# Cross attention on one core: two groups of Q ahead of a tile of V, the mask turned one tile later, and the last products by row blocks

## What is computed

```
qh = split_heads(q @ wq.T + bq)
kh = split_heads(k @ wk.T + bk)
vh = split_heads(v @ wv.T + bv)
scores = einsum('ntd,nsd->nts', qh, kh) / sqrt(depth) + mask * PAD
ctx = einsum('nts,nsd->ntd', softmax(scores), vh)
out = merge_heads(ctx) + q
out = (out - mean(out)) / sqrt(var(out) + 1e-5) * gamma + beta
```

## Time and profile before

| | |
|---|---|
| median of 3 runs | 1091.9 us (1089.82 to 1092.0) |
| the profiled execution | 1091.3 us |
| its span | 1089.2 us |
| TensorE products busy | 1064.5 us, 98% |
| VectorE busy | 939.8 us, 86% |
| GpSimd busy | 773.8 us, 71% |
| ScalarE busy | 725.4 us, 67% |

### The profile page before, as it was taken

How to read it: one execution, slowest core, us unless ns; L and a number is a source line. 1 busy time by engine, 2 the same in 40 slices (tenths; PEclk the granted TensorE clock), 3 DMA queues, 4 the chain that set the end, 5 groups by cost and what they waited for, 6 DMA issues and landing times.

```text
span 1089.2 us, 27000 instructions
## 1 busy us (share of the span) xinstructions
PE 1064.5 (98%) x7541; PEld 978.4 (90%) x7541; DVE 939.8 (86%) x1778; ACT 725.4 (67%) x1149; POOL 773.8 (71%) x685
## 2 busy tenths in 40 slices
PE   7999899999999999999999999999999999999995
PEld 7888789999999999999999999999999999999994
DVE  5989878888888898888888888888888888888897
ACT  3331566777777777777777777777777777777674
POOL 3999723776777777777777777777777777777687
PEclk9999999999999999999999999999999999999998
DMA  7664645465565565555566566566555556556444
...
DMA packets 176905, 171.32 MB, mean 157 GB/s; under 512 B 110004, under 2 KB 111556, under 8 KB 176868
## 3 DMA queue, kind: packets, MB, share of 16 engines
...
...
## 4 chain that ended last, share of the span: by engine, by line
PE 85%; POOL 7%; DVE 4%; issue 1%; DMA 1%; ACT 1%; SPq 1%; DVEq 0%; ACTq 0%; POOLq 0%
PE q_ps L950 33%; PE o_ps L1035 24%; PE t_ps L998 13%; PE s_ps L982 11%; PE s_ps L985 4%; POOL k_part L323 2%; POOL k_shift L319 2%; POOL v_out L335 1%; PE o_ps L965 1%; DMA keep_h<-in_mask 1%; POOL x_lo L354 0%; DVE stats L1107 0%; POOL wq_lo L350 0%; DVE row_max L1173 0%; DVE attn L1099 0%
## 5 line engine op out<-in xcount | busy, mean ns | idle before, releaser
L1035 PE MATMUL o_ps<-v_tiles,pt 128*128 128x66 f32 x2500 | 307.3, 270 | 0.5 <-DVE attn L1099 0.5
L1035 PEld LDWEIGHTS o_ps<-v_tiles,pt 128*128 128x128 f32 x2500 | 298.7, 192 | 0.9 <-issue 0.9
L1426 ACT COPY pt<-t_ps 128x512 f32<-128x512 f32 x315 | 184.0, 584 | 153.2 <-PE t_ps L998 150.2
L1173 DVE TENSOR_REDUCE row_max<-s_ps 128x8 f32<-128x616 f32 x256 | 204.6, 799 | 91.2 <-PE s_ps L985 80.3
L1302 POOL TENSOR_TENSOR x_lo<-xT_raw,x_hi 128x512 fp32r<-128x512 f32 x120 | 153.3, 1278 | 178.7 <-ACT x_hi L1399 178.0
L1389 ACT ACTIVATE probs<-probs 128x616 f32<-128x616 f32 x256 | 184.2, 720 | 82.5 <-DVE probs L1182 76.8
L950 PE MATMUL q_ps<-x_lo,wq_hi 128*128 128x512 f32 x496 | 221.2, 446 | 0.0
L1260 POOL TENSOR_TENSOR attn<-attn,v_late 128x512 f32<-128x512 f32 x124 | 159.5, 1287 | 74.4 <-DVE attn L1099 74.2
L1182 DVE TENSOR_TENSOR probs<-s_ps,row_max 128x616 f32<-128x616 f32 x256 | 204.6, 799 | 5.8
L950 PE MATMUL q_ps<-x_hi,wq_hi 128*128 128x512 f32 x496 | 195.7, 395 | 0.0
L950 PE MATMUL q_ps<-x_hi,wq_lo 128*128 128x512 f32 x496 | 195.5, 394 | 0.0
...
## 6 DMA issues: line engine op xcount, KB each, us to landing
xT_raw<-in_xT SPq DMA_DIRECT2D x128, 256.0 KB, 3.5
...
k_scratch<-k_out SPq DMA_DIRECT2D x8, 1232.0 KB, 5.5
...
```

Source lines behind the costliest of these rows:

```text
L1035: mm = pe.matmul(bank_of(b, t)[:, col:col + tile_cols[i]], pt_of(b, h)[0:w, i, P * t:P * t + P], v_tiles[v_buffer(b, h)][0:w, i, 0:tile_co ...
L1173: dve.tensor_reduce(row_max[:, u, :].rearrange("p (j h) -> p j h", j=2), score_heads(t), AX.X, ALU.max).then_inc(max_ready, 1)
L1426: act.copy(pt[h][0:w, i, :], t_ps[0:w, :]).then_inc(pt_ready, 1)
```

## The change

Three things are moved, and one is joined.

1. `turn_keep` comes behind value tile 1 of chunk 0 instead of tile 0.
2. On TensorE the first two groups of Q of batch 0 come ahead of the last chunk's value tile, and take the banks of groups 48 and 49 instead of 52 and 53. ScalarE reads them out ahead of the casts of key tiles 28 and 29, issues the moves there, and makes x's high parts between the last casts. VectorE makes Q's first low parts behind the low part of tile 28.
3. In the tail the two halves of a row block follow each other (`in_turn`), half 0 in one bank and half 1 in the other (`bank_of`).
4. The row factors of batch 30 are computed once for its four row blocks. ScalarE copies x into PSUM ahead of the normalizations.

```diff
+def first_group(g):
+    return CHUNKS * GROUPS + g - (VT - LATE if g < 2 else 0)
-    return bank(CHUNKS * GROUPS + g)
+    return bank(first_group(g))
...
             n = (2 * c + half) * NG + m
-            if n == 2 * NG * CHUNKS - 1:
+            behind_end = 2 * NG * CHUNKS - n
+            if behind_end == 4:
                 first_high(0)
+            if behind_end == 3:
                 first_high(1)
                 move_first_half()
+            if behind_end == 2:
+                second_x(0)
+                second_x(1)
+            if behind_end == 1:
+                second_x(2)
+                second_x(3)
             act.wait_ge(k_ready, n + 1)
...
+    def second_x(k):
+        if k == 0:
+            act.wait_ge(k_done, 2 * NG * CHUNKS)
+        act.wait_ge(xT_loaded[k], 2 * DMA)
+        act.copy(x_hi1[:, k, :], xT_raw[:, k, :]).then_inc(x_hi_ready, 1)
...
-    act.wait_ge(k_done, 2 * NG * CHUNKS)
-    for k in range(KC):
-        act.wait_ge(xT_loaded[k], 2 * DMA)
-        act.copy(x_hi1[:, k, :], xT_raw[:, k, :]).then_inc(x_hi_ready, 1)
     first_high(2)
...
-        for j in range(VT if c < CHUNKS - 1 else LATE):
+        if c == CHUNKS - 1:
+            last_values(c)
+            return
+        for j in range(VT):
             bias_values(c, j)
             if j < NG:
                 low_keys_out(2 * c * NG + NG + j)
-        if c < CHUNKS - 1:
-            return
-        for j in range(LATE, NG):
-            if j == NG - 1:
-                for g in range(2):
-                    first_low(g)
-            low_keys_out(2 * c * NG + NG + j)
+    def last_values(c):
+        first = 2 * c * NG + NG
+        bias_values(c, 0)
+        low_keys_out(first)
+        first_low(0)
+        first_low(1)
+        low_keys_out(first + 1)
+        low_keys_out(first + 2)
         for k in range(2):
             dve.wait_ge(x_hi_ready, KC + k + 1)
             dve.tensor_tensor(x_lo1[:, k, :], xT_raw[:, k, :], x_hi1[:, k, :], ALU.subtract
                               ).then_inc(x_lo_ready, 1)
+        low_keys_out(first + 3)
...
-        wait_for_bank(pe, CHUNKS * GROUPS + g)
+        wait_for_bank(pe, first_group(g))
...
         ctx_part = (ctx_hi[c % 2], ctx_lo[c % 2])
+        if c == CHUNKS - 1:
+            for g in range(2):
+                first_queries(g)
...
-            if (c, j) == (0, 0):
+            if (c, j) == (0, 1):
                 turn_keep()
-    for g in range(NG):
+    for g in range(2, NG):
         first_queries(g)
...
-def bank_of(b, t):
-    return t_ps if is_last(b) and t % 2 == 0 else o_ps
+def bank_of(b, h):
+    return t_ps if is_last(b) and h == 0 else o_ps
+def in_turn(b, h, t):
+    return 2 * t + h if is_last(b) else 4 * h + t
...
         if is_last(b):
-            u = 4 * h + t
+            u = in_turn(b, h, t)
             if u > 0:
                 pe.wait_ge(attn_ready, b * 8 + (u - 1))
...
     tail_turn(0)
     product(LAST, 0, 0)
     tail_turn(1)
-    product(LAST, 0, 1)
-    product(LAST, 0, 2)
-    product(LAST, 0, 3)
-    tail_turn(2)
-    product(LAST, 1, 0)
-    tail_turn(3)
-    for t in range(1, TT):
+    for t in range(TT):
         product(LAST, 1, t)
+        if t + 1 < TT:
+            product(LAST, 0, t + 1)
+        if t + 2 < TT:
+            tail_turn(t + 2)
...
     read_out(LAST - 1, 1, 3, 1 - LAST_PAR)
     read_out(LAST, 0, 0, LAST_PAR)
-    read_out(LAST, 0, 1, LAST_PAR)
-    tail_stats(LAST - 1, 2, 1 - LAST_PAR)
-    read_out(LAST, 0, 2, LAST_PAR)
-    tail_stats(LAST - 1, 3, 1 - LAST_PAR)
-    read_out(LAST, 0, 3, LAST_PAR)
+    for t in range(2, TT):
+        tail_stats(LAST - 1, t, 1 - LAST_PAR)
     for t in range(TT):
         read_out(LAST, 1, t, LAST_PAR)
         add_last_row(t)
+        if t + 1 < TT:
+            read_out(LAST, 0, t + 1, LAST_PAR)
         tail_stats(LAST, t, LAST_PAR)
...
     add_rows(LAST - 1, 3, 1 - LAST_PAR)
-    tail_factors(LAST - 1, 0, 2, 3)
-    scale_rows(LAST - 1, 0, 1 - LAST_PAR)
-    tail_factors(LAST - 1, 2, 4, 4)
-    scale_rows(LAST - 1, 1, 1 - LAST_PAR)
-    scale_rows(LAST - 1, 2, 1 - LAST_PAR)
+    tail_factors(LAST - 1, 0, TT, 3)
+    for t in range(TT - 1):
+        scale_rows(LAST - 1, t, 1 - LAST_PAR)
...
     copy_tail(0)
     exponent(LAST, 1, 3)
     copy_tail(1)
-    norm(LAST - 1, 0, 1 - LAST_PAR)
     x_into_bank(0)
     x_into_bank(1)
     copy_tail(2)
+    norm(LAST - 1, 0, 1 - LAST_PAR)
     copy_tail(3)
-    norm(LAST - 1, 1, 1 - LAST_PAR)
     x_into_bank(2)
     x_into_bank(3)
+    norm(LAST - 1, 1, 1 - LAST_PAR)
     norm(LAST - 1, 2, 1 - LAST_PAR)
     norm(LAST - 1, 3, 1 - LAST_PAR)
```

28 lines of the change are left out of this document (13 added, 15 removed).

## The result

The changed kernel takes 1094.1 us in the median (1093.0 to 1096.2, 19 runs), against 1091.2 for the kernel before on the same chip: a ratio of 1.0034, 95% interval 1.0028 to 1.0040, so +3.7 us by the ratio (3.1 to 4.4), slower. A twentieth run, of 2135.0 us, was in a slow state and is left out. The prediction was 1091.5, with a range to 1093.8: the time lies outside it. The profiled executions give a span of 1092.4 against 1089.2: +3.2.

The account below looks back on a forecast made before the run. TensorE was taken to bound the kernel, with 85% of the chain. First stage -0.5 and tail +0.25 gave -0.25 us: 1091.65 against the 1091.9 median, 1091.05 against the profiled execution, put at 1091.5, range 1088.4 to 1093.8.

Parts of the forecast that it names:

- The mask: First chunk: TensorE's 1.27 us gap before the mask's transposes goes; VectorE, ScalarE and GpSimd do not get ahead.
- Q before V's tile: End of the first stage, TensorE: Q0 and Q1 lose the 1.15 us wait, Q2 waits until 113.8, Q3 ends at 119.4.
- The three moves: Moves of Q, first stage's end: last lands at 118.3; first scores near 119.45 instead of 123.72, at full clock.
- The port: SBUF port of VectorE and GpSimd: GpSimd's string first, VectorE stands 119.1 to 121.9, tile 31's low part ends 124.2.
- The landing of the store: Store of the last keys: issued at 124.25, landing 5.4 us later alone, up to 6.2; 0.3 added for Q's second moves.
- a rival: The slower rival, 13%: the store of the last keys lands 0.9 us later, besides a fall of the clock.
- My third late tile at 137.6: TensorE's third late tile of V, now at 138.34, starts at 137.6, leaving 0.75 of the 5.8 us gained.
- My -0.5: First stage's net gain: 0.75 us left, less 0.3 for the slower store, gives -0.5 us; between -0.75 and 0.0.
- Who waits for the store, and that the columns of ones bind: First stage's end: GpSimd's clearing and ones wait for the landing; VectorE's bias follows at 131.35, 0.7 later than now.
- The tail: Last products: VectorE's statistics 1.6 us earlier, GpSimd's block 1 rows 0.67 later; sum +0.25 us, between -0.35 and +0.7.
- A: At the port VectorE goes first: bias 128.8 to 129.8, third late tile 135.0 to 136.0, time 1089.3; 24%.
- B: Clock falls in the 1.75 us wait before the third late tile or in the other two; up to 1094.3; 13%.

Follow-up runs that it names:

- e6_hold_store: Changed kernel with SyncE's store of the first half of the last keys held until Q's first three moves landed: 1092.1 us, 1.0025 of the kernel before.
- e9_port: Changed kernel with GpSimd's two low parts of x waiting until the last key tile's low part is written: 1091.2 us, 1.0016 of the kernel before.
- e4_hold_x: Changed kernel with SyncE's load of x of batch 2 held until both halves of the last keys landed: 1092.2 us, 1.0016 of the kernel before.
- e7_ones: Changed kernel with GpSimd's columns of ones written ahead of the clearing of the three value tiles: 1092.7 us, 1.0018 of the kernel before.
- t2_joint: Kernel before with the joint factor and ScalarE's new order of normalizations, last products as before: 1091.9 us, 1.0011 of the kernel before.

## Why the prediction was wrong, step by step

- **The mask: right.** The gap went, and what waits behind it took most of the gain.
- **Q before V's tile, on TensorE: right.** Q2 started at 113.57 for 113.8, with a wait of 0.76, and Q3 ended where it should.
- **The three moves: wrong.** I took "today's 2.4 us from its issue" for the last. Today's moves leave 5 us behind the store of the first half of the last keys (114.97 and 119.87); moved forward they leave beside it, and the last took 6.3. e6_hold_store shows both numbers. So the first scores came 2.7 later than forecast, and the clock fell, which I had at 1.00. In e6_hold_store the third late tile gets 2.1 us back, not by the earlier scores but by the second moves, which are then out of the way of the store of the last keys.
- **The port: right in place and size, wrong in order.** I expected GpSimd's string first and then all of VectorE's; two low parts of keys slipped in ahead and the others took turns. Store issued 123.66, forecast 124.25 (the five operations behind 121.9 add up to 124.35 for the end of the last, where I wrote 124.2). e9_port gives the price.
- **The landing of the store: wrong, the term that failed.** I put it between 5.4 and 6.2, with 5.7 in the sum, and 0.9 more only in a rival; it was 8.1. The load of x of batch 2 I had at nothing. SyncE issues it right behind the store once the low parts of x are there, and these came earlier by the change itself: before, GpSimd's ended at 126.48 and the load left at 126.57, now it leaves at 124.56. e4_hold_x puts 1.9 us on it. The second moves of Q I had counted, at 0.3; with them beside it and the load held, the store takes 6.2 us, 0.8 over the 5.4 (e4_hold_x); with the load beside it and the moves 1.4 us ahead it takes 6.5, 1.6 under the 8.1 (e6_hold_store). My third late tile at 137.6 was worked out with 5.4. The store issued 0.6 earlier than forecast and landing 2.7 later give +2.1, and that is by how much the tile came later (139.73); against the sum, which had 0.25 more, it is 1.9. My -0.5 turns into +1.4.
- **Who waits for the store, and that the columns of ones bind: right.** e7_ones.
- **The tail: wrong, +0.25 for +1.2.** The step was that block 1's normalization "must follow the copy at 1072.69". I left the copy of turn 3 where it was; in the new order that turn stands behind more products and a wait for the third value tile, and the copy starts at 1075.75, less the 2.0 by which all is later, 1.1 later. The gap that this leaves on GpSimd, 1.15 us, is the larger part of the 1.6 by which its last factors are later within the tail. And I called the joint factor nothing, since GpSimd "now waits anyway"; it makes block 0 late, by 0.45 us here, and by itself the tail 2.0 longer in t2_joint.
- **The rivals.** A (VectorE first at the port) did not come in the changed kernel. e9_port is A made by hand: its bias at 128.73 is as A had it, but the first scores wait for the slow moves until 122.03, the clock falls there (0.50 from 124 to 126), and the third late tile comes at 136.79, where A had 135.0 to 136.0. B named a fall of the clock behind the wait of the third late tile: there were 1.18 us and no fall; it fell at the first scores. That its 1094.3 lies near the result is luck. That the change in its two halves is a loss in both I had at no chance of its own.
